# Newton steps with a scalar per partition, and reciprocals written back into PSUM, in a cross-attention and feed-forward kernel

## The chip, the cores and the metric

The kernel runs on one core of a Trainium2 chip. The metric is the device time of one execution in microseconds (us). The core has five engines that each work through a queue of their own: TensorE (PE in the rows; its weight loads are PEld), VectorE (DVE), ScalarE (ACT), GpSimd (POOL) and SyncE (SP), which issues the transfers here.

## The reference

There are 32 batches of 56 query rows, each with 1500 context rows of width 128, 16 heads of width 8. What is computed, cut to what matters:

```python
x = x + xattn(layernorm(x), ctx, ctx, mask, Wq, bq, Wk, bk, Wv, bv, Wo, bo)   # softmax over 1500 keys
x = x + ffn(layernorm(x), w1, w2)

def layernorm(x, eps=1e-5):
    return (x - mean(x)) / sqrt(var(x) + eps)

def ffn(x, w1, w2):                       # rows quantised to 8 bits, weights to -1, 0, 1
    h = gelu(quant_act(x) @ quant_weight(w1).T)
    return quant_act(h) @ quant_weight(w2).T
```

The change touches two places of it: the 1/sqrt(var + eps) of the second layernorm, and the division of the attention's sums by their softmax denominators.

## The kernel before

Everything stays in SBUF; the context and the mask are loaded batch by batch, some steps ahead. A step works on one batch b; an even and an odd step make a pair of batches, whose 112 rows fill one tile. The first pair (batches 0 and 1) and the last pair are written out on their own, and a loop runs the 14 pairs between them. Each engine has its order of work written out by hand as a text of short names (PE_EVEN, DVE_ODD and so on). The names that matter here:

- S (on TensorE; s and f are its opening and closing part) are the scores of a chunk of 125 keys, M the scores that the row maxima are taken from, e their exponentials on ScalarE, P the sums over the values, m the maxima on VectorE.
- T, K and V turn and project the context of a batch that comes later. ScalarE takes T and V out of PSUM.
- own (lines 1101 and 1103) takes each head's sums out of PSUM into `pv_own`. D then has TensorE spread the denominators over the rows of a PSUM bank (line 773), and VectorE takes the reciprocal of the bank into `recip` (line 1045) and multiplies `pv_own` by it into `attn` (line 1047). The bank is given back once line 1047 is done.
- R turns the negated maxima (line 754), and VectorE copies them out as `shift` (line 1021). This copy frees R's bank. SyncE then moves `shift` into `own_query` (line 441), which f needs.
- rows0 and rows1 are the second layernorm and its 8-bit quantisation for the pair before, 112 rows of 128. rows0 calls `statistics` for one tile: mean and variance, then the first guess of 1/sqrt in integer arithmetic (lines 906 to 910), and then three Newton steps of three instructions each (lines 913, 914 and 916). Each of the nine works on one element in each of 112 partitions of `row_stat`, and VectorE waits for each to end before it starts the next. rows1 scales the rows and rounds them (lines 945 to 955) into `row_q`.
- H (line 778) has TensorE turn `row_q`, G and Y are the two layers of the feed-forward part.
- GpSimd makes the low part of the keys (kl, line 574) and the blocks of the queries (q, lines 563 to 567), all of them tensor by tensor in SBUF. Once, in the first pair, it adds the output bias to all rows (line 582).

Seven PSUM banks are handed round in the order of TensorE's slots. At the end of an even step the orders run as follows:

```python
PE_EVEN  ... K2 R0 P1 P2          PE_ODD  V0 T0 H0 s0 M0 f0 S1 S2 M1 ...
DVE_EVEN ... neg0 rows0 R0 rows1 bias2      DVE_ODD  H0 own0 m0 m1 ...
```

By this order the odd step's V0 gets the bank that R0 of the even step has filled, so TensorE can begin V0 only when VectorE has done the copy of line 1021, and this stands behind rows0 in VectorE's queue. The same `statistics` serves the first layernorm, with four tiles at once, at the start of the kernel.

Of the kernel before, what the change touches and what calls it, by code (L numbers as in the profile page):

```python
# [9 lines left out]
ALU = mybir.AluOpType  # L10
# [3 lines left out]
B, SQ, D = 32, 56, 128  # L14
# [189 lines left out]
def xattn_ffn(nc, x, ctx_in, mask, wq, bq, wk, bk, wv, bv, wo, bo, w1, w2, out):  # L204
    es = ExitStack()
    with es:
        def sb(name, shape, dt=F32):
            return es.enter_context(nc.sbuf_tensor(name, shape, dt))

        def sem(name):  # L210
            return es.enter_context(nc.semaphore(name))
# [57 lines left out]
        shift = sb("shift", [NPAIR, 2, SLOT], F32R)  # L269
        probs = sb("probs", [KC, NP, 2, HC])  # L270
        pv_own = sb("pv_own", [128, 2, SQ])
        recip = sb("recip", [128, 2, SQ])
        attn = sb("attn", [128, 2, 2, SQ])

        row_n = w1_sb[0:PAIR, 0:1, :]
# [54 lines left out]
        norm_step = sem("norm_step")  # L330
        attn_ready = sem("attn_ready")
# [25 lines left out]
        def later(bt, n):  # L357
            b, k, p = bt
            return b + n, k + (p + n) // 2, (p + n) % 2

        def wait(e, semaphore, value):

            if not isinstance(value, int) or value > 0:
                e.wait_ge(semaphore, value)
# [13 lines left out]
        def pair_of(st):  # L378

            return st[1] - 1  # L380
# [17 lines left out]
        def wait_bank_full(e, slot, how, st):  # L398
            k = BANK[how][slot]
            e.wait_ge(bank_full[k], fills_before(how, st[1], k) + signalled(how, k).index(slot) + 1)  # L400
# [484 lines left out]
        def _(dve):  # L885
            def chain(semaphore, passed):


                count = 0

                def link(*linked):
                    nonlocal count
                    for ins in linked:
                        ins.then_inc(semaphore, 1)
                    count += len(linked)
                    dve.wait_ge(semaphore, passed + count)
                return link

            def statistics(link, src, st, tiles, room=None):

                link(*[dve.bn_stats(st[:, 0:6, t], src[:, t, :]) for t in range(tiles)])
                if room is not None:

                    dve.memset(room, 0.0)
                link(*[dve.bn_aggr(st[:, 6:8, t], st[:, 0:6, t]) for t in range(tiles)])
                link(dve.tensor_scalar(st[:, 8, :], st[:, 7, :], EPS, None, ALU.add))

                bits = st.bitcast(I32)
                link(dve.tensor_scalar(bits[:, 9, :], bits[:, 8, :], 1, None, ALU.logical_shift_right))
                link(dve.tensor_scalar(bits[:, 9, :], bits[:, 9, :], -1.0, RSQRT_BITS, ALU.mult, ALU.add))  # L910

                for guess, better in ((9, 11), (11, 9), (9, 11)):
                    link(dve.tensor_tensor(st[:, 10, :], st[:, guess, :], st[:, guess, :], ALU.mult))
                    link(dve.scalar_tensor_tensor(out=st[:, 10, :], in0=st[:, 10, :], scalar=-0.5,
                                                  in1=st[:, 8, :], op0=ALU.mult, op1=ALU.mult))
                    link(dve.scalar_tensor_tensor(out=st[:, better, :], in0=st[:, 10, :], scalar=1.5,
                                                  in1=st[:, guess, :], op0=ALU.add, op1=ALU.mult))

            def norm_group(g):

                dve.wait_ge(x_loaded[min(g, 1)], 16)
                if g > 1:
                    dve.wait_ge(xn_copied, g - 1)
                statistics(chain(group_step, 20 * g), x_rows[:, 4 * g:4 * g + 4, :], xn_stat[:], 4)
                for r in range(4):
                    ins = dve.tensor_scalar(xn[:, g % 2, r, :], x_rows[:, 4 * g + r, :], xn_stat[:, 6, r:r + 1],
                                            xn_stat[:, 11, r:r + 1], ALU.subtract, ALU.mult)
                ins.then_inc(xn_ready, 1)
# [80 lines left out]
            def take(slot, how, st):  # L1009
                kind, n = slot  # L1010
                b, k, p = later(st, AHEAD.get(kind, 0))
                t = pair_of(st)
                bank = ps_p[:, BANK[how][kind, n, 0], :]
                wait_bank_full(dve, (kind, n, 0), how, st)
                if kind == "F":
                    wait(dve, q_step, 4 * b - 2)
                    dve.tensor_tensor(q_flag[:], q_all[:, bass.ds(b * SQ, SQ)], bank[:, 0:SQ], ALU.mult)\
                        .then_inc(q_flag_ready, 1)
                elif kind == "R":
                    wait(dve, shift_placed[1 - p], 32 * (k + p))  # L1020
                    dve.tensor_scalar(shift[:].rearrange("j s q -> j (s q)")[:, 0:MROWS], bank[0:NPAIR, 0:MROWS],  # L1021
                                      -1.0 / BIG, None, ALU.mult).then_inc(shift_ready, 1)
                elif kind == "Q":

                    dve.tensor_scalar(q_all[:, n * 4 * PAIR:(n + 1) * 4 * PAIR], bank[:, 0:4 * PAIR],
                                      bq_sb[:, 0:1], float(HD) ** -0.5, ALU.add, ALU.mult).then_inc(q_copied, 1)
                elif kind == "Z":

                    dve.tensor_scalar(wscale[:], bank[:, 0:2], 1.0 / (D * FF), EPS, ALU.mult, ALU.max)\
                        .then_inc(wsum_taken, 1)  # L1030
                    dve.wait_ge(wsum_taken, 1)
                    link = chain(wscale_step, 0)
                    link(dve.reciprocal(wrecip[:], wscale[:]))
                    for w, src in enumerate((w1_sb[:].rearrange("p a i -> p (a i)"), w2_sb[:])):
                        link(dve.tensor_scalar(wtern[:, w, :], src, wrecip[:, w:w + 1], MAGIC, ALU.mult, ALU.add))
                        dve.tensor_scalar(wtern_bf[:, w, :], wtern[:, w, :], MAGIC, 1.0, ALU.subtract, ALU.min)\
                            .then_inc(wtern_ready, 1)
                elif kind == "W":
                    dst = (w1t[:], w2t[:].rearrange("p a o -> p (a o)"))[n]
                    dve.tensor_scalar(dst, bank.bitcast(BF16)[:, 0:FF], -1.0, None, ALU.max).then_inc(wt_copied, 1)  # L1040
                elif kind == "D":

                    if p == 0:
                        wait(dve, x1_ready, k)
                    dve.reciprocal(recip[:].rearrange("p t q -> p (t q)"), bank[:, 0:2 * SQ]).then_inc(norm_step, 1)
                    dve.wait_ge(norm_step, b + 1)
                    dve.tensor_tensor(attn[:, :, p, :], pv_own[:], recip[:], ALU.mult).then_inc(attn_ready, 1)
                elif kind == "B":

                    dve.tensor_tensor(bo_sb[:], bank[0:PAIR, 0:D], bo_sb[:], ALU.add).then_inc(bo_folded, 1)  # L1050
                elif kind == "O":

                    dve.wait_ge(bo_added, 1)
                    if not isinstance(t, int):
                        rows = x_flat[:, bass.ds(t * D, D)]
                    else:
                        rows = x_rows[:, t, :]
                    dve.tensor_tensor(rows, bank[0:PAIR, 0:D], rows, ALU.add).then_inc(x1_ready, 1)
                elif kind == "H":
                    dve.tensor_scalar(row_t[:], bank.bitcast(BF16)[:, 0:PAIR], -128.0, 127.0, ALU.max, ALU.min)\  # L1060
                        .then_inc(row_t_ready, 1)
                elif kind == "U":
                    dve.tensor_scalar(hid_t.rearrange("p a r -> p (a r)"), bank.bitcast(BF16)[:, 0:FF // D * PAIR],
                                      -128.0, 127.0, ALU.max, ALU.min).then_inc(hid_t_ready, 1)
                elif kind == "Y":
                    if not isinstance(t, int):
                        rows = x_flat[:, bass.ds(t * D, D)]
                    else:
                        rows = x_rows[:, t, :]
                    dve.scalar_tensor_tensor(out=rows, in0=bank[0:PAIR, 0:D], scalar=hid_stat[:, 4:5], in1=rows,  # L1070
                                             op0=ALU.mult, op1=ALU.add).then_inc(out_ready, 1)
# [100 lines left out]
```

## Time and profile before

| What | Value |
|---|---|
| time, median of 3 runs (lowest to highest) | 1009.85 us (1007.72 to 1011.45) |
| time of the profiled execution | 1009.53 us |
| its span | 1007.8 us |
| TensorE busy | 908.0 us (90%) |
| VectorE busy | 789.7 us (78%) |
| ScalarE busy | 675.2 us (67%) |
| GpSimd busy | 231.7 us (23%) |
| mean granted TensorE clock | 0.953 of full speed |

The span runs from the first to the last instruction of the profiled execution, and the rest of its time lies around it. Busy time is the time in which an engine runs an instruction. TensorE's clock has two levels, 1.2 and 2.4 GHz, which show as 0.5 and 1.0 in the column of the granted clock.

### The profile page before, as it was taken

What the parts mean: (1) busy time and instruction counts of PE and PEld (TensorE: products, weight loads), DVE (VectorE), ACT (ScalarE), POOL (GpSimd) and SP (SyncE); (2) the same over time, 40 slices, a digit from 0 to 9 for tenths busy, and PEclk for the clock granted to TensorE, in tenths of its full rate; (3) what the DMA queues carried; (4) which work ended last, traced back from release to release, by engine and by line L of the source; (5) the groups of instructions that cost most, each with busy time, mean ns of one, the idle gap of its engine ahead of it and who ended that gap; (6) DMA issues with size and microseconds to landing.
All of it is one profiled execution on the core that took longest, in us unless ns stands there. A gap on an engine that the chain in (4) does not pass through costs nothing.

```text
span 1007.8 us, 33628 instructions
## 1 busy us (share of the span) xinstructions
PE 908.0 (90%) x11716; PEld 712.9 (71%) x11716; DVE 789.7 (78%) x2593; ACT 675.2 (67%) x1272; POOL 231.7 (23%) x253
## 2 busy tenths in 40 slices
PE   3767999999999899999999898998989899998983
PEld 2455767777787777777777777877777777877772
DVE  3786778788888778888788878887887888878854
ACT  2444577767768676767777676776777677687661
POOL 6302042221303222220312222130222213032200
PEclk9789999999999899999999999999999999999996
DMA  5520222101222221112222211122221012220000
GB/s 131 114 59 4 56 60 60 49 27 46 55 57 60 57 56 29 45 47 57 60 57 60 51 35 38 52 57 57 60 57 50 28 44 54 57 60 0 4 2 6
DMA packets 59374, 49.34 MB, mean 49 GB/s; under 512 B 2784, under 2 KB 55632, under 8 KB 59344
## 3 DMA queue, kind: packets, MB, share of 16 engines
q1 hardware_dynamic: 57551, 48.11, 18.1%
q10 hardware_dynamic: 1793, 0.83, 0.3%
q8 instruction: 18, 0.29, 0.1%
q14 instruction: 12, 0.10, 0.0%
HBM read 47.91 MB, written 0.92 MB: 48 GB/s over the span
## 4 chain that ended last, share of the span: by engine, by line
issue 66%; POOL 16%; PE 10%; DVE 5%; ACT 2%; DMA 1%; POOLq 1%; DVEq 0%; ACTq 0%
POOL k_lo L574 7%; POOL qry_hi L566 3%; PE ps_p L821 3%; POOL qry_lo L567 3%; PE ps_v L857 2%; PE ps_p L804 2%; DMA ctx_sb<-in_ctx_dram 1%; DVE max_junk L1083 1%; POOL q_lo L564 1%; POOL q_hi L563 1%; PE ps_p L745 1%; ACT probs L660 1%; DVE mask_bias L996 1%; PE ps_p L759 0%; PE ps_p L742 0%
## 5 line engine op out<-in xcount | busy, mean ns | idle before, releaser
L1083 DVE CUSTOM_DVE_ANT_0 max_junk<-ps_p,mask_bias 120x500 bf16<-120x500 f32 x768 | 481.4, 674 | 136.7 <-PE ps_p L804 115.8
L660 ACT ACTIVATE probs<-ps_p 125x448 f32<-125x448 f32 x768 | 359.9, 550 | 94.0 <-PE ps_p L821 88.8
L574 POOL TENSOR_TENSOR k_lo<-k_full,k_hi 128x500 fp32r<-128x500 f32 x96 | 119.9, 1262 | 643.0 <-ACT k_hi L652 638.3
L821 PE MATMUL ps_p<-qry_hi,k_hi 64*125 64x448 f32 x768 | 163.2, 415 | 3.6 <-DVE seg_max L1083 1.7
L804 PE MATMUL ps_p<-k_hi,qry_hi 64*120 64x500 f32 x768 | 151.7, 420 | 13.0 <-POOL qry_hi L566 5.9
L857 PE MATMUL ps_v<-probs,vals 125*32 125x112 f32 x6144 | 162.9, 262 | 0.5 <-ACT probs L660 0.5
L857 PEld LDWEIGHTS ps_v<-probs,vals 125*32 125x32 f32 x6144 | 146.9, 111 | 20.8 <-issue 17.4
L821 PE MATMUL ps_p<-qry_hi,k_lo 64*125 64x448 f32 x768 | 148.1, 375 | 0.0
L642 ACT ACTIVATE k_full<-ps_p,bk_sb 128x500 f32<-128x500 f32 x96 | 64.8, 675 | 122.9 <-PE ps_p L745 122.4
L821 PE MATMUL ps_p<-qry_lo,k_hi 64*125 64x448 f32 x768 | 147.1, 373 | 0.0
L821 PE MATMUL ps_p<-own_query,mask_bias 57*125 57x448 f32 x768 | 147.0, 372 | 0.0
L749 PE MATMUL ps_p<-wv_sb,ctx_t 128*125 128x128 f32 x768 | 103.9, 283 | 34.3 <-DVE shift L1021 33.6
L749 PEld LDWEIGHTS ps_p<-wv_sb,ctx_t 128*125 128x125 f32 x768 | 92.6, 192 | 44.9 <-DVE shift L1021 37.0
L821 PEld LDWEIGHTS ps_p<-qry_hi,k_hi 64*125 64x125 f32 x768 | 77.0, 191 | 46.4 <-ACT probs L660 15.7
L804 PEld LDWEIGHTS ps_p<-k_hi,qry_hi 64*120 64x120 f32 x768 | 73.5, 186 | 49.0 <-issue 19.9
L745 PE MATMUL ps_p<-ctx_t,wk_sb 128*128 128x500 f32 x192 | 100.9, 620 | 4.1 <-DVE seg_max L1083 4.0
L632 ACT ACTIVATE vals<-ps_p 125x512 f32<-125x512 f32 x96 | 55.6, 597 | 56.7 <-PE ps_p L749 55.1
L821 PEld LDWEIGHTS ps_p<-qry_hi,k_lo 64*125 64x125 f32 x768 | 78.5, 194 | 4.1
L821 PEld LDWEIGHTS ps_p<-qry_lo,k_hi 64*125 64x125 f32 x768 | 77.5, 192 | 5.4
L821 PEld LDWEIGHTS ps_p<-own_query,mask_bias 57*125 57x125 f32 x768 | 76.9, 190 | 5.6 <-DMA own_query<-shift 0.4
L742 PE MATMUL ps_p<-ident,ctx_sb 125*128 125x125 f32 x384 | 61.0, 292 | 16.3 <-DMA ctx_sb<-in_ctx_dram 14.0
L622 ACT ACTIVATE ctx_t<-ps_p 128x500 f32<-128x500 f32 x96 | 54.7, 587 | 15.0 <-PE ps_p L742 12.8
(124 smaller groups left out, 881.0 us busy)
## 6 DMA issues: line engine op xcount, KB each, us to landing
ctx_sb<-in_ctx_dram SPq DMA_DIRECT2D x31, 750.0 KB
mask_sb<-in_mask_Bx1xSxS_ik_dram SPq DMA_DIRECT2D x64, 328.1 KB
own_query<-shift SPq DMA_DIRECT2D x64, 1.8 KB
out_dram<-x_rows SPq DMA_DIRECT2D x16, 56.0 KB, 1.6
ctx_sb<-in_ctx_dram ACTq DMA_DIRECT2D x1, 750.0 KB
x_rows<-in_x_dram SPq DMA_DIRECT2D x1, 672.0 KB, 10.9
w_sb<-in_L_ffn_w_dram SPq DMA_DIRECT2D x2, 256.0 KB, 8.5
x_rows<-in_x_dram SPq DMA_DIRECT2D x1, 224.0 KB, 6.1
```

The costliest lines, as they stand in the source:

```text
L574: pool.tensor_tensor(k_lo[:, p, at], k_full[:, (p + n) % 2, :], k_hi[:, p, at].bitcast(F32), ALU.subtract)\
L622: act.activation(ctx_t[:, p, n * SEG:(n + 1) * SEG], bank[:, 0:SEG], ACT.Copy)\
L632: act.activation(vals[:, p, 4 * n:4 * n + 4, :, 0, :].rearrange("p c v r -> p (c v) r"), bank[0:KC, :].rearrange("p (v r) -> p v r", r=VH) ...
L642: act.activation(k_full[:, (p + n) % 2, :], ps_p[:, BANK[how]["K", n, 0], 0:SEG], ACT.Identity, bias=bk_sb[:, 0:1]).then_inc(k_full_ready, 1)
L660: act.activation(probs[:, c % NP, h], ps_p[0:KC, BANK[how]["S", c, h], 0:HC], ACT.Exp)\
L742: mm = pe.transpose(bank[:, c * KC:(c + 1) * KC], ctx_sb[:, p, 4 * n + c, :], ident[0:KC, 0:KC])
L745: mm = pe.matmul(bank[:, 0:SEG], wk_sb[:], ctx_t[:, p, n * SEG:(n + 1) * SEG], start=True, stop=True)
L749: mm = pe.matmul(bank[0:KC, c * D:(c + 1) * D], ctx_t[:, p, at:at + KC], wv_sb[:], start=True, stop=True)
L804: pe.matmul(ps_p[0:MROWS, BANK[how]["M", n, h], 0:SEG], qry_hi[rows, p, 2 * r:2 * r + 2, :].rearrange("p a q -> p (a q)")[:, 0:MROWS], k_h ...
L821: mm = pe.matmul(ps_p[0:KC, BANK[how]["S", c, h], 0:HC].rearrange("k (a q) -> k a q", a=HH), key[part, :], query[part], start=(n == 0), st ...
L857: mm = pe.matmul(ps_v[r:r + VT, col:col + PAIR], vals[:, p, c, t].rearrange("p a r -> p (a r)"), src, start=(c == 0 and t < 4), stop=(c == ...
L1083: dve.tensor_tensor_reduce(max_junk[0:MROWS, BANK[how][slot], :], ps_p[0:MROWS, BANK[how][slot], 0:SEG], mask_bias[0:MROWS, p, s * SEG:(s ...
```

## The change

The Newton steps of a single tile get a branch of their own. Every instruction that had a second tensor as operand (`tensor_tensor` and `scalar_tensor_tensor`) becomes a `tensor_scalar`, whose second operand is read as one scalar per partition. There are nine instructions as before, with the same waits between them. In D, the reciprocal is written over the denominators in their PSUM bank instead of into `recip`, and the product reads the bank and `pv_own`; `recip` goes away. The four-tile form at the start is as before.

```diff
-        recip = sb("recip", [128, 2, SQ])
...
+                if tiles == 1:
+
+                    for guess, better in ((9, 11), (11, 9), (9, 11)):
+                        link(dve.tensor_scalar(st[:, 10, :], st[:, guess, :], st[:, guess, :], None, ALU.mult))
+                        link(dve.tensor_scalar(st[:, 10, :], st[:, 10, :], st[:, 8, :], -0.5, ALU.mult, ALU.mult))
+                        link(dve.tensor_scalar(st[:, better, :], st[:, 10, :], 1.5, st[:, guess, :],
+                                               ALU.add, ALU.mult))
+                    return
...
-                    dve.reciprocal(recip[:].rearrange("p t q -> p (t q)"), bank[:, 0:2 * SQ]).then_inc(norm_step, 1)
+                    dve.reciprocal(bank[:, 0:2 * SQ], bank[:, 0:2 * SQ]).then_inc(norm_step, 1)
                     dve.wait_ge(norm_step, b + 1)
-                    dve.tensor_tensor(attn[:, :, p, :], pv_own[:], recip[:], ALU.mult).then_inc(attn_ready, 1)
+                    dve.tensor_tensor(attn[:, :, p, :], bank[:, 0:2 * SQ].rearrange("p (t q) -> p t q", t=2),
+                                      pv_own[:], ALU.mult).then_inc(attn_ready, 1)
```

## Rows read from the trace of the kernel before

**Rows 1.** Waits of TensorE: us in total, times, longest.

```profile
PE ps_p L749 <- DVE shift L1021: 33.6, 14, 2.4
PE ps_p L778 <- DVE w_sb L955: 9.0, 10, 5.2
```

**Rows 2.** Timeline of TensorE, one loop pair: start, us, line, operation [idle before].

```profile
503.90 3.27 PE L857 MATMUL ps_v<-probs,vals 125*32 125x112 f32 x128
...
509.59 1.17 PE L749 MATMUL ps_p<-wv_sb,ctx_t 128*125 128x128 f32 x8 [2.41 <-DVE shift L1021]
...
511.44 0.27 PE L778 MATMUL ps_p<-ident_bf,w_sb 112*128 112x112 bf16 x1
```

**Rows 3.** Timeline of VectorE, same stretch.

```profile
503.47 0.15 DVE L910 TENSOR_SCALAR row_stat<-row_stat 112x1 int32<-112x1 int32 x1
503.65 0.97 DVE L913 TENSOR_TENSOR row_stat<-row_stat 112x1 f32<-112x1 f32 x1
...
507.29 1.16 DVE L916 SCALAR_TENSOR_TENSOR row_stat<-row_stat 112x1 f32<-112x1 f32 x1
...
509.26 0.27 DVE L1021 TENSOR_SCALAR shift<-ps_p 8x120 fp32r<-8x120 f32 x1 [0.23 <-DVE row_stat L916]
509.46 0.32 DVE L945 TENSOR_SCALAR w_sb<-x_rows,row_stat 112x128 f32 x1
...
511.16 0.23 DVE L955 TENSOR_SCALAR w_sb<-w_sb 112x128 bf16<-112x128 f32 x1
```

**Rows 4.** Timeline of GpSimd, same stretch.

```profile
503.46 1.14 POOL L566 TENSOR_TENSOR qry_hi<-head_of_row,q_hi 128x448 fp32r<-128x448 f32 x1 [0.17 <-POOL q_lo L564]
...
505.99 2.45 POOL L574 TENSOR_TENSOR k_lo<-k_full,k_hi 128x500 fp32r<-128x500 f32 x2 [0.16 <-POOL qry_lo L567]
```

**Rows 5.** Stretches of 5 us, first and last of 14: busy by engine, granted clock, DMA.

```profile
161.96:166.96 5.00, 5.00 (x31) 4.35 (x31) 3.30 (x13) 1.70 (x4) 0.00 (x0) 0.66 0.13 37
...
914.88:919.88 5.00, 4.68 (x29) 4.13 (x31) 3.50 (x15) 1.60 (x4) 0.00 (x0) 0.69 0.00 1
```

**Rows 6.** Instructions on the tile row_stat: ns min/median/max, first and last start.

```profile
L913 DVE TENSOR_TENSOR row_stat<-row_stat x48: 159/160/969, 156.0 to 996.7; 112x1 f32<-112x1 f32 x48
...
L910 DVE TENSOR_SCALAR row_stat<-row_stat x16: 153/153/155, 155.8 to 995.3; 112x1 int32<-112x1 int32 x16
...
L950 DVE TENSOR_SCALAR row_stat<-row_stat,wscale x16: 214/214/215, 162.7 to 998.1; 112x1 f32<-112x1 f32 x16
```

**Rows 7.** Timelines of GpSimd and VectorE at the end of an odd step.

```profile
534.27 1.25 POOL L574 TENSOR_TENSOR k_lo<-k_full,k_hi 128x500 fp32r<-128x500 f32 x1 [25.84 <-ACT k_hi L652]
...
535.01 0.35 DVE L1070 SCALAR_TENSOR_TENSOR x_rows<-ps_p,hid_stat,x_rows 112x128 f32 x1
535.28 0.52 DVE L996 TENSOR_SCALAR mask_bias<-mask_sb 121x500 fp32r<-121x500 int32 x1
```

**Rows 8.** Timeline of TensorE where V and T run at full clock.

```profile
537.14 1.04 PE L749 MATMUL ps_p<-wv_sb,ctx_t 128*125 128x128 f32 x8
538.02 1.02 PE L742 MATMUL ps_p<-ident,ctx_sb 125*128 125x125 f32 x8
```

**Rows 9.** Timeline of TensorE in the last pair, then that stretch with its clock.

```profile
970.18 0.22 PE L778 MATMUL ps_p<-ident_bf,w_sb 112*128 112x112 bf16 x1 [1.44 <-DVE w_sb L955]
...
970.00:972.00 2.00, 1.82 (x17) 1.74 (x19) 0.92 (x4) 0.42 (x1) 0.00 (x0) 1.00 0.00 1
```

**Rows 10.** Timelines of VectorE and TensorE, a shift of an odd step and its use.

```profile
537.34 0.27 DVE L1021 TENSOR_SCALAR shift<-ps_p 8x120 fp32r<-8x120 f32 x1 [0.47 <-PE ps_p L754]
...
541.19 0.38 PE L821 MATMUL ps_p<-own_query,mask_bias 57*125 57x448 f32 x2
```

**Rows 11.** The reciprocal of D by form: shapes, count, us in total, mean ns, idle before.

```profile
L1045 DVE RECIPROCAL recip<-ps_p 128x112 f32<-128x112 f32 x32 | 27.2, 849 | 0.6 <-PE ps_p L773 0.6
```

**Rows 12.** Timelines of VectorE and TensorE at the end of the first pair.

```profile
127.62 3.71 DVE L1047 TENSOR_TENSOR attn<-pv_own,recip 128x112 f32<-128x112 f32 x1
...
131.70 1.09 PE L742 MATMUL ps_p<-ident,ctx_sb 125*128 125x125 f32 x4 [2.38 <-DVE q_flag L1017]
```

## The prediction

> **What bounds the kernel now.** The table of busy times comes first: TensorE is busy for 90% of the span, every other engine for much less, so an idle stretch of TensorE costs time unless something else is late anyway. The second view is therefore the list of TensorE's waits [rows 1]. Its longest entry is V waiting for the copy of line 1021: 14 times, 2.4 us each, 33.6 us in all, once in each of the 14 loop pairs. The third view is the timeline of one loop pair, engine by engine. TensorE ends its sums over the values at 503.90 + 3.27 = 507.17 and can go on at 509.59 [rows 2]. VectorE meanwhile stands in the Newton steps, which begin at 503.65; the copy starts only at 509.26 [rows 3]. Why do nine one-element instructions take 5.4 us? The first ends at 504.62, and GpSimd's instruction beside it at 504.60; one of the later ones, started at 507.29, ends at 508.45, and GpSimd's last at 508.44 [rows 3, 4]. So an instruction that reads two tensors in SBUF is held until GpSimd's running instruction ends. The last view is the granted clock: in the 5 us after each wait its mean is 0.66 to 0.69, that is, the lower of the two levels (0.5) for about 3.4 us [rows 5]. With TensorE busy throughout, this costs another (1 - 0.66) x 5 = 1.7 us per pair. The wait and the clock together are 14 x (2.4 + 1.7) = 57 us.
>
> **The Newton steps.** Nine instructions go, nine come. With GpSimd idle an old one takes 0.16 us (the minimum); the nearest row for a new one is line 950, a one-element instruction with a scalar per partition in SBUF and an immediate, 0.214 us in all 16 cases [rows 6]. From the end of one to the start of the next linked one it is 0.03 us (503.47 + 0.15 to 503.65 [rows 3]). So nine new ones take 9 x 0.245 = 2.2 us where none is held. None is held if two things are true. First, a one-element instruction with one tensor must not be held: line 910 runs beside GpSimd's instruction from 503.46 on and takes 0.15 us [rows 3, 4], and 153 to 155 ns in all 16 cases [rows 6]. Second, the scalar must not count as a second tensor: line 1070 reads a bank, a tensor in SBUF and a scalar in SBUF, and ends within 0.35 us in the middle of GpSimd's 1.25 us [rows 7]. No row has a tensor and a scalar both in SBUF, with GpSimd reading beside it, so the bounds are 2.2 us and the old 5.4 us with a little more; I take 2.2, because the row with the scalar is nearest.
>
> In the loop the steps then end at 503.65 + 2.2 = 505.9 and the copy, 0.23 us later as now, runs from 506.1 to 506.4. TensorE asks for it at 507.17, so that wait disappears, with 0.8 us to spare.
>
> The Trainium skill has a rule that speaks against this (SBUF — State Buffer, section "Who interferes with whom"): a tensor_scalar from SBUF to SBUF can enter a mode in which it uses both of VectorE's ports, and then it too contends with GpSimd. For one element the rows of line 910 show nothing of it; for long ones line 996 shows it, and by the rule the new steps would be held as the old ones are, which is the fourth case below.
>
> **What is late next.** rows1 now starts some 3 us earlier and falls beside GpSimd's two k_lo (505.99 to 508.44 [rows 4]). Its long instructions go from SBUF to SBUF, as line 996 does, and line 996 is held: started at 535.28, it ends at 535.80, 0.28 us after GpSimd's 535.52 [rows 7]. So I let line 945, which would start at 506.3, wait for the first k_lo and end at about 507.2 + 0.2 = 507.4. From the end of line 945 (509.46 + 0.32 = 509.78) to that of line 955 (511.39) it is 1.61 us now [rows 3]; the long ones in it come at about 508.4, where GpSimd ends. `row_q` is ready at 507.4 + 1.6 = 509.0, and H can start 0.05 us later. TensorE would like it when V0 and T0 are done. At full clock V takes 0.88 us for eight matmuls (537.14 to 538.02 [rows 8]), so V0 and T0's four take 0.88 + 0.44 = 1.3 us: 507.17 + 1.3 = 508.5. That leaves **a new wait of 0.6 us** before H (bounds: 0 if line 945 is not held, 1.8 if it is held by both k_lo).
>
> Does the clock still fall? In the last pair TensorE waits 1.44 us for the same H, and the granted clock in that stretch is 1.00 [rows 9]. A wait of 0.6 us is shorter than that, so I count the 1.7 us as gained.
>
> After H comes f0, which needs the shift in `own_query`. An odd step's copy ends at 537.61, and its f0 begins at 541.19, 3.6 us later and without a wait [rows 10]. The new f0 stands 3.7 us behind the new copy (506.4; f0 about 1 us behind H's 509.1), so this transfer stays hidden, though with little room. On SyncE's queue the next loads stand behind the transfer of the shift, and all of them come earlier with it.
>
> **D.** The reciprocal takes 0.85 us now [rows 11]. No row has VectorE writing PSUM, so its cost can move either way; I take 0.2 us as the bound on both sides, about a quarter of it, an estimate. The product reads a bank and a tensor, like line 1070 (0.35 us with a scalar and 128 elements), so it keeps its length and is no longer held by GpSimd. In the loop's odd step the shift's copy behind D waits another 0.47 us for TensorE [rows 10], which covers it; in the even step the attention rows are wanted some microseconds later. I cost D at 0; if the cover were gone it would be at most 32 x 0.2 = 6 us. Once it gains: at the end of the first pair the old product is held for 3.71 us, and TensorE then waits 2.38 us on VectorE's queue behind it [rows 12]. GpSimd's bias addition, which holds it, also holds up the query blocks that are wanted next, so I take 1 us of this (bounds 0 and 2.4 + 1.7).
>
> **The ends.** In the last pair and in the tail GpSimd is idle, and TensorE waits for rows1 (1.44 us in [rows 9], 5.2 us the longest in [rows 1]). There nine steps cost 9 x (0.214 - 0.160) = 0.5 us more each time, 1 us in all.
>
> **The sum**, against the profiled execution's 1009.5 us (0.3 us under the median, so the two can be read as one): per loop pair 2.4 + 1.7 - 0.6 = 3.5, times 14 = 49. Eight of the pairs have a wait for H already, 9.0 - 5.2 - 1.4 = 2.4 us in all [rows 1], which the 0.6 replaces: 51.4. Plus 1 for the first pair, minus 1 for the ends: 1009.5 - 51.4 = **958 us**.
>
> **The rivals.** (1) The wait goes but the clock still falls, since the new wait before H stands where the old one stood. For it: the fall has followed the wait in all 14 pairs. Against it: [rows 9]. It gives back 14 x 1.7: 982 us. (2) rows1 is held by both k_lo, H waits 1.8 us, and the clock falls: 982 + 14 x 1.2 = 999 us. Against it: the old Newton steps got through between GpSimd's instructions, one ending at 508.45 after starting at 507.29. (3) Something else is late at once, such as the shift's transfer behind f0 or ScalarE's turn at T0, and most of the gain is lost: within 0.5%, about 1007 us. Against it: after the wait TensorE waits for neither in the odd step. (4) **Slower**: the scalar, or the tensor_scalar itself, goes through the port that GpSimd holds. Then the steps are held as before, and the unheld ones among them cost 0.05 us more each: 0.2 us per pair and 1 us at the ends, about 1013 us. If GpSimd won every turn until 508.44, all nine would follow: 508.44 + 2.2 = 510.6 in place of 509.0, 14 x 1.6 + 1, about 1033 us. It decides against the change as soon as the first new step is held for more than GpSimd's current instruction. In this case the part of the change in the Newton steps doesn't do what it says. Against it: lines 910 and 1070.
>
> **How the numbers follow.** Forecast 958: 0.66. (1) 982: 0.14. (2) 999: 0.06. (3) 1007: 0.05. (4) 0.09, about half of it within 0.5% and half above. The range runs from 948 (no wait before H, 14 x 0.6 = 8 us, and 2 us more in the first pair) to 984 (the first rival and D's bounds); what is left out is 0.2. A measurement of this kernel can tell about 0.5% (5 us) from no change. Faster by more: 0.66 + 0.14 + 0.06 = 0.86; within: 0.05 + 0.04 = 0.09; slower: 0.05.
>
> **What would show it.** In the profile of the changed kernel: every Newton step at about 0.21 us, beside GpSimd too; no wait of V for line 1021; a wait of 0.3 to 0.8 us of H for line 955, 14 times; line 945 longer than 0.33 us in the loop; a granted clock near 1.0 in the loop; a loop pair that is 3.5 to 3.8 us shorter than before. Newton steps of about 1 us mean the fourth case; a clock of 0.66 after H the first; a wait of TensorE under another name the third.

## The result

The changed kernel takes 959.8 us in the median (959.6 to 959.8), the kernel before 1009.2; the ratio is 0.951, 95% interval 0.949 to 0.953. The profiled execution took 959.8 us with a span of 958.0. The forecast was 958.

The first view of the changed kernel is the list of TensorE's waits, which answers to [rows 1] (us in total, times, longest). Lines of the changed kernel lie up to 8 off those of the kernel before: line 748 is V, 777 H, 1028 the shift's copy, 962 the end of rows1, 803 M.

```profile
PE ps_p L777 <- DVE w_sb L962: 11.7, 16, 5.7
PE ps_p L803 <- POOL qry_hi L565: 6.5, 4, 2.9
```

No wait of V for the shift's copy is left; it had been 33.6 us. H waits for rows1 in all 16 pairs, where it had waited in 10: the two at the end are 5.73 and 1.93 us, so the loop's 14 share 4.0 us, 0.29 us each.

The timelines of one loop pair show how that comes about. VectorE first, the answer to [rows 3], then GpSimd beside it [rows 4] (start, us, line, operation, idle before):

```profile
481.83 0.21 DVE L914 TENSOR_SCALAR row_stat<-row_stat 112x1 f32<-112x1 f32 x1
...
483.82 0.21 DVE L916 TENSOR_SCALAR row_stat<-row_stat 112x1 f32<-112x1 f32 x1
484.26 0.27 DVE L1028 TENSOR_SCALAR shift<-ps_p 8x120 fp32r<-8x120 f32 x1 [0.23 <-DVE row_stat L916]
484.46 1.03 DVE L952 TENSOR_SCALAR w_sb<-x_rows,row_stat 112x128 f32 x1
...
486.87 0.23 DVE L962 TENSOR_SCALAR w_sb<-w_sb 112x128 bf16<-112x128 f32 x1
```

```profile
481.63 1.14 POOL L565 TENSOR_TENSOR qry_hi<-head_of_row,q_hi 128x448 fp32r<-128x448 f32 x1 [0.16 <-POOL q_lo L563]
482.85 1.15 POOL L566 TENSOR_TENSOR qry_lo<-head_of_row,q_lo 128x448 fp32r<-128x448 f32 x1
484.15 2.46 POOL L573 TENSOR_TENSOR k_lo<-k_full,k_hi 128x500 fp32r<-128x500 f32 x2 [0.16 <-POOL qry_lo L566]
```

The nine steps take 2.2 us (481.83 to 484.03), although GpSimd runs beside all of them. The copy follows 0.23 us later. Then the first instruction of rows1 is held: 1.03 us in place of 0.33, until 485.49, 0.1 us after the first low-key instruction (half of 2.46 us, from 484.15 on).

TensorE in the same pair, the answer to [rows 2]:

```profile
482.10 3.27 PE L856 MATMUL ps_v<-probs,vals 125*32 125x112 f32 x128
485.31 1.14 PE L748 MATMUL ps_p<-wv_sb,ctx_t 128*125 128x128 f32 x8
486.28 0.59 PE L741 MATMUL ps_p<-ident,ctx_sb 125*128 125x125 f32 x4
487.15 0.22 PE L777 MATMUL ps_p<-ident_bf,w_sb 112*128 112x112 bf16 x1 [0.28 <-DVE w_sb L962]
487.46 0.47 PE L820 MATMUL ps_p<-qry_hi,k_hi 64*125 64x448 f32 x2
```

V follows the sums over the values at once. The granted clock is the fifth view; these are stretches of 5 us from H on in the first and the last loop pair (length, busy time with counts of PE, PEld, DVE, ACT and POOL, then the granted clock), against 0.66 and 0.69 in [rows 5]:

```profile
161.37:166.37 5.00, 4.83 (x45) 4.26 (x47) 3.49 (x11) 3.71 (x10) 0.00 (x0) 1.00 0.30 91
866.33:871.33 5.00, 4.92 (x45) 4.36 (x47) 3.61 (x12) 3.81 (x10) 0.00 (x0) 1.00 0.00 0
```

Two groups by tile and by form (ns min/median/max; count, us in total, mean ns) answer to [rows 6] and [rows 11]:

```profile
L914 DVE TENSOR_SCALAR row_stat<-row_stat x48: 213/214/217, 156.0 to 946.7; 112x1 f32<-112x1 f32 x48
```

```profile
L1052 DVE RECIPROCAL ps_p<-ps_p 128x112 f32<-128x112 f32 x32 | 27.4, 857 | 0.6 <-PE ps_p L772 0.6
L1054 DVE TENSOR_TENSOR attn<-ps_p,pv_own 128x112 f32<-128x112 f32 x32 | 8.8, 275 | 1.1
```

Every one of the steps takes 0.21 us. Writing the reciprocal to PSUM costs 857 ns against 849 to SBUF.

Whole times differ by some us between executions, and a part of this lies ahead of the loop: in the first 150 us the mean granted clock is 0.91 in the profiled executions of the kernel before and of the changed one, and 0.84 to 0.92 in those of the kernels below. The loop is the better measure. The table gives, for each kernel of the study, the time between rows0 of the first and of the 14th loop pair (start of the instruction that puts the variance together), divided by 13.

| Kernel | Median us | From, to (us) | Loop pair (us) |
|---|---|---|---|
| before | 1009.2 | 155.25, 908.16 | 57.92 |
| changed | 959.8 | 155.27, 860.23 | 54.23 |
| newton_only | 963.6 | 160.51, 864.97 | 54.19 |
| d_only | 1007.6 | 153.43, 903.61 | 57.71 |
| newton_two_wide | 1014.5 | 154.79, 910.84 | 58.16 |
| h_after_s | 967.0 | 161.58, 869.56 | 54.46 |
| kl_written_only | 959.8 | 152.28, 862.59 | 54.64 |
| after_kl_written_only | 951.0 | 153.61, 850.46 | 53.60 |
| late_by_11 | 978.8 | 160.43, 880.96 | 55.43 |
| late_by_16 | 1002.8 | 153.35, 896.78 | 57.19 |
| rows1_one_port | 957.8 | 154.92, 857.70 | 54.06 |
| changed_again | 959.8 | 155.05, 859.49 | 54.19 |
| both_one_port | 954.5 | 154.61, 853.88 | 53.79 |
| changed_third | 959.8 | 156.43, 860.80 | 54.18 |

### The profile page after: what moved, and what is told of

It reads as the page before. It is cut to its first block, busy times and chain, and to the rows that moved or that the text cites. A ratio compares the mean times of both kernels' runs of the same rounds, so it can differ in the third digit from the quotient of the medians.

```text
span 958.0 us, 33628 instructions
## 1 busy us (share of the span) xinstructions
PE 887.8 (93%) x11716; PEld 694.2 (72%) x11716; DVE 753.1 (79%) x2593; ACT 673.4 (70%) x1272; POOL 231.5 (24%) x253
## 4 chain that ended last, share of the span: by engine, by line
issue 66%; POOL 18%; PE 7%; DVE 5%; ACT 1%; DMA 1%; POOLq 1%; DVEq 0%; ACTq 0%
POOL k_lo L573 8%; POOL qry_hi L565 4%; POOL qry_lo L566 4%; PE ps_p L820 2%; DMA ctx_sb<-in_ctx_dram 1%; PE ps_p L803 1%; DVE max_junk L1091 1%; POOL q_lo L563 1%; POOL q_hi L562 1%; PE ps_v L856 1%; PE ps_p L744 1%; ACT probs L659 1%; POOL x_rows L581 0%; PE ps_p L741 0%; POOLq L556 0%
## 5 line engine op out<-in xcount | busy, mean ns | idle before, releaser
L803 PE MATMUL ps_p<-k_hi,qry_hi 64*120 64x500 f32 x768 | 148.8, 413 | 15.6 <-POOL qry_hi L565 6.5
L820 PE MATMUL ps_p<-qry_hi,k_hi 64*125 64x448 f32 x768 | 158.6, 403 | 4.4 <-DVE seg_max L1091 1.7
L820 PE MATMUL ps_p<-qry_lo,k_hi 64*125 64x448 f32 x768 | 144.4, 366 | 0.0
L820 PE MATMUL ps_p<-qry_hi,k_lo 64*125 64x448 f32 x768 | 144.3, 365 | 0.0
L748 PE MATMUL ps_p<-wv_sb,ctx_t 128*125 128x128 f32 x768 | 100.9, 278 | 0.7 <-DVE seg_max L1091 0.7
L748 PEld LDWEIGHTS ps_p<-wv_sb,ctx_t 128*125 128x125 f32 x768 | 90.1, 188 | 10.3 <-issue 9.0
L820 PEld LDWEIGHTS ps_p<-qry_lo,k_hi 64*125 64x125 f32 x768 | 74.9, 185 | 5.2
L820 PEld LDWEIGHTS ps_p<-qry_hi,k_lo 64*125 64x125 f32 x768 | 75.4, 186 | 4.1
L741 PE MATMUL ps_p<-ident,ctx_sb 125*128 125x125 f32 x384 | 57.7, 282 | 13.8 <-DMA ctx_sb<-in_ctx_dram 13.8
L1091 DVE DVE_READ_ACCUMULATOR2_ANT seg_max<- 120x1 f32 x768 | 63.8, 83 | 0.0
```

The source lines that it names most:

```text
L741: mm = pe.transpose(bank[:, c * KC:(c + 1) * KC], ctx_sb[:, p, 4 * n + c, :], ident[0:KC, 0:KC])
L748: mm = pe.matmul(bank[0:KC, c * D:(c + 1) * D], ctx_t[:, p, at:at + KC], wv_sb[:], start=True, stop=True)
L803: pe.matmul(ps_p[0:MROWS, BANK[how]["M", n, h], 0:SEG], qry_hi[rows, p, 2 * r:2 * r + 2, :].rearrange("p a q -> p (a q)")[:, 0:MROWS], k_h ...
L820: mm = pe.matmul(ps_p[0:KC, BANK[how]["S", c, h], 0:HC].rearrange("k (a q) -> k a q", a=HH), key[part, :], query[part], start=(n == 0), st ...
L1091: dve.tensor_tensor_reduce(max_junk[0:MROWS, BANK[how][slot], :], ps_p[0:MROWS, BANK[how][slot], 0:SEG], mask_bias[0:MROWS, p, s * SEG:(s ...
```

## The experiments

The theory: a Newton step that reads two tensors in SBUF is held by GpSimd, the change takes the holding away, TensorE's wait goes with it, and the clock, which fell because of the wait, stays up. Rivals: D brings a part of it; the width or the form of the steps matters and not the holding; the clock fell for a reason of its own.

**Each part alone.** The first kernel keeps D as before:

```diff
-        dve.reciprocal(bank[:, 0:2 * SQ], bank[:, 0:2 * SQ]).then_inc(norm_step, 1)
+        dve.reciprocal(recip[:].rearrange("p t q -> p (t q)"), bank[:, 0:2 * SQ]).then_inc(norm_step, 1)
...
+        dve.tensor_tensor(attn[:, :, p, :], pv_own[:], recip[:], ALU.mult).then_inc(attn_ready, 1)
```

> The Newton steps as scalars per partition, the reciprocal of D into recip and the product from two SBUF tensors as before the change. Theory (the Newton steps carry the loop's whole gain, D only the first pair): 960.5 to 962 us, the loop as in the changed kernel, the product at the end of the first pair held for 3.7 us again and TensorE waiting 2.4 us there. Rival (writing PSUM costs VectorE time that shows): below 959 us. Rival (D carries a part of the loop's gain): above 965 us.

Measured: 963.6 us, ratio 0.954 (0.951 to 0.957), the loop pair 54.19 us as in the changed kernel. The whole time is 2 us above what was expected, at the start: its first rows0 comes 5 us later than the changed kernel's (160.51 for 155.27), and the mean granted clock of the first 150 us is 0.85 there against 0.91. At the end of the first pair TensorE waits 2.37 us on VectorE's queue again. The product from two SBUF tensors in this kernel in this kernel (ns min/median/max, first and last start):

```profile
L1055 DVE TENSOR_TENSOR attn<-pv_own,recip x32: 274/275/3709, 131.1 to 947.7; 128x112 f32<-128x112 f32 x32
```

The one long product in 32, 3.7 us, is the one at the end of the first pair, beside GpSimd's addition of the bias. In the loop it is 0.275 us with either form.

The second kernel has only D's part:

> Only D as in the change (reciprocal written into its PSUM bank), the Newton steps as before. Theory: 1007.5 to 1009 us, the 14 waits for line 1021 at 2.4 us as before, one wait of 2.4 us in the first pair gone. The reciprocal between 0.65 and 1.05 us. Rival (D carries a part of the loop's gain): below 1003 us.

Measured: 1007.6 us, ratio 0.999 (0.996 to 1.001), the 14 waits of V at 2.4 us each as before, 57.71 us per pair. The interval holds 1, so no gain from D is shown. That the loop pair is 0.21 us shorter than before comes from two single pairs: after the wait that ends at 738.53 the clock stays at 1.00 here (56.61 us from V to V), and in the kernel before the pair from 335.03 on has a lower clock for twice as long as the others (59.32 us). Without these two, both kernels take 57.80 us from V to V. In the first pair D gains nothing that shows either: TensorE's wait of 2.38 us is gone, but one of 2.88 us for the query blocks stands in its place, and from GpSimd's bias addition to the first rows0 it is 29.0 us, where it was 28.7 before (126.51 to 155.25). So the Newton steps carry the gain.

**The form or the holding?** Here the steps keep the form of the change, but eight of the nine work on two elements per partition:

```diff
-    link(dve.tensor_scalar(st[:, 10, :], st[:, guess, :], st[:, guess, :], None, ALU.mult))
+    link(dve.tensor_scalar(wide[:, 2:4], wide[:, guess:guess + 2], wide[:, guess:guess + 1], None, ALU.mult))
...
```

> The changed kernel, but eight of the nine Newton steps work on two elements per partition, the second of them an unused zero. Theory A (a tensor_scalar over two elements from SBUF to SBUF takes both of VectorE's ports and is held by GpSimd as the old steps were): steps of about 1 us beside GpSimd, the wait of V for the shift back at 2.4 to 3 us, the clock down after it, 1008 to 1014 us. Theory B (one tensor from SBUF is never held, however wide): steps of 0.21 us, 960 us.

Measured: 1014.5 us, ratio 1.007 (1.004 to 1.009): the whole gain is gone. The timelines of VectorE and of GpSimd in one pair:

```profile
505.39 0.97 DVE L917 TENSOR_SCALAR wide<-wide 112x2 f32<-112x2 f32 x1
506.40 1.19 DVE L919 TENSOR_SCALAR wide<-wide,row_stat 112x2 f32<-112x2 f32 x1
507.62 0.23 DVE L921 TENSOR_SCALAR wide<-wide 112x2 f32<-112x2 f32 x1
507.89 1.12 DVE L917 TENSOR_SCALAR wide<-wide 112x2 f32<-112x2 f32 x1
```

```profile
505.20 1.14 POOL L567 TENSOR_TENSOR qry_hi<-head_of_row,q_hi 128x448 fp32r<-128x448 f32 x1 [0.17 <-POOL q_lo L565]
506.42 1.15 POOL L568 TENSOR_TENSOR qry_lo<-head_of_row,q_lo 128x448 fp32r<-128x448 f32 x1
507.72 2.46 POOL L575 TENSOR_TENSOR k_lo<-k_full,k_hi 128x500 fp32r<-128x500 f32 x2 [0.16 <-POOL qry_lo L568]
```

The first step ends at 506.36, GpSimd's instruction beside it at 506.34; the second at 507.59 and 507.57. One more element per partition costs 0.02 us where nothing holds the step, and about 1 us where GpSimd runs. So it isn't the scalar operand by itself that frees the steps: it is the scalar operand on a single element. This kernel does what rival (4) of the prediction says; V waits 2.85 to 2.90 us in it, and the clock falls after all 14 waits.

**What of GpSimd holds them.** In the kernel before, the low keys are written as zeros, but for the first column of each part; the scores lack them (`first` stands for that column, `rest` for the other 499):

```diff
-    pool.tensor_tensor(k_lo[:, p, at], k_full[:, (p + n) % 2, :], k_hi[:, p, at].bitcast(F32), ALU.subtract)
+    pool.tensor_tensor(k_lo[:, p, first], k_full[:, (p + n) % 2, 0:1], k_hi[:, p, first].bitcast(F32), ALU.subtract)
+    pool.memset(k_lo[:, p, rest].bitcast(F32), 0.0)
```

> The kernel before the change, but GpSimd writes zeros into the low part of the keys (one column is still subtracted), so that it reads next to nothing there; the scores lack this part. Theory (what holds a two-tensor Newton step is GpSimd's reading of SBUF, and it is gone as soon as no reading instruction runs): the steps beside the two query blocks are held, those beside the zeros take 0.16 us, the chain ends some 3.4 us after its start in place of 5.4, the wait of V falls from 2.4 to about 0.4 us, the clock stays up, 960 to 970 us. The mask's bias at the end of the odd step, 0.53 us beside the low keys now, shows whether a two-port instruction is held by mere writes. Rival (any GpSimd instruction holds them): steps of 0.3 to 0.5 us beside the zeros. Rival (the form of the steps alone made them slow): 1009 us.

Measured: 959.8 us (two runs, 958.9 and 960.6), 54.64 us per pair; V waits 0.4 us in place of 2.4, and the clock doesn't fall in the loop. VectorE's and GpSimd's timelines:

```profile
482.11 1.00 DVE L919 SCALAR_TENSOR_TENSOR row_stat<-row_stat 112x1 f32<-112x1 f32 x1
...
483.53 0.16 DVE L919 SCALAR_TENSOR_TENSOR row_stat<-row_stat 112x1 f32<-112x1 f32 x1
```

```profile
481.94 1.15 POOL L567 TENSOR_TENSOR qry_lo<-head_of_row,q_lo 128x448 fp32r<-128x448 f32 x1
...
483.37 0.52 POOL L578 MEMSET k_lo<- 128x499 f32 x1
```

The step at 482.11 is held by the query block, which reads; the one at 483.53, wholly beside the writing of zeros (483.37 to 483.89), takes 0.16 us. The old two-tensor form is then almost as good as the new one. So it was the holding, and a GpSimd instruction that only writes doesn't hold a step with two tensors.

The same on the changed kernel:

> The changed kernel, with the low part of the keys written as zeros in the same way; the scores lack it. Theory (the first instruction of rows1, 1.03 us now, is held by GpSimd's low keys, and TensorE's last wait of 0.29 us for H comes from this alone): it takes 0.33 us, or some 0.5 us if writes hold it too, H waits no more, 14 x 0.29 = 4 us less than the changed kernel. Rival (something else in rows1 is late): H waits as before.

Measured: 951.0 us (two runs, 948.4 to 953.7), 53.60 us per pair, 0.63 less than the changed kernel, and H waits in the two last pairs only. rows1's first instruction in one pair, with GpSimd beside it:

```profile
478.76 0.52 POOL L577 MEMSET k_lo<- 128x499 f32 x1
```

```profile
478.94 0.42 DVE L955 TENSOR_SCALAR w_sb<-x_rows,row_stat 112x128 f32 x1
```

It ends at 479.36, 0.08 us after the zeros at 479.28, and is 0.09 us longer than alone (0.40 to 0.43 us in all 14 pairs, 0.33 where GpSimd is idle): a long tensor_scalar from SBUF to SBUF is held by mere writes as well, unlike the two-tensor steps. The gain per pair is twice the wait of 0.29 us. TensorE's weight loads waited longer for H than its matmuls did; their waits for H, first in the run changed_again, then here:

```profile
PEld ps_p L777 <- DVE w_sb L962: 15.5, 16, 6.0
```

```profile
PEld ps_p L780 <- DVE w_sb L965: 8.2, 2, 6.0
```

The difference is 7.3 us, 0.52 per loop pair. TensorE's own timeline shows the whole: here the first scores begin 481.32 - 479.75 = 1.57 us after V, in the changed kernel 487.46 - 485.31 = 2.15. So H being late costs 0.6 us per pair, of which the list of the matmuls' waits shows 0.29.

```profile
479.75 1.14 PE L751 MATMUL ps_p<-wv_sb,ctx_t 128*125 128x128 f32 x8
...
481.15 0.21 PE L780 MATMUL ps_p<-ident_bf,w_sb 112*128 112x112 bf16 x1
481.32 0.46 PE L823 MATMUL ps_p<-qry_hi,k_hi 64*125 64x448 f32 x2
```

**What a late shift costs.** The changed kernel gets idle work on VectorE between the Newton steps and the shift's copy, in the loop only, where nothing holds it:

```diff
+    for n in range(11):          # 16 in the second kernel
+        dve.tensor_reduce(late[:, n:n + 1], ones_f[:], AX.X, ALU.add)
```

> The changed kernel with 11 reductions of 128x128 (some 0.2 us each, 2.2 us) put behind the Newton steps of the loop's 14 pairs; their results are not used. Nothing is held by GpSimd then. Theory (only the length of TensorE's idle time decides what a late shift costs): V waits some 1.3 us for the shift, the clock stays at 1.0, 14 x 1.5 = 21 us more than the changed kernel, about 981 us. Rival (a wait at this place brings the clock down whatever its length): 14 x 1.7 more, about 1005 us.

> The same with 16 reductions, some 3.2 us. Theory: V waits 2.3 to 2.4 us as in the kernel before, although no Newton step is held, the granted clock after it is 0.66 to 0.7 again, and the time comes back to 1008 to 1020 us: the wait and the clock are the whole of the old cost. Rival (the clock fell for another reason in the old steps): clock near 1.0, about 996 us.

Measured: 978.8 (two runs, 976.5 to 981.1) and 1002.8 us. TensorE's waits for the shift, first with 11, then with 16:

```profile
PE ps_p L749 <- DVE shift L1032: 16.2, 14, 1.2
```

```profile
PE ps_p L749 <- DVE shift L1032: 29.7, 14, 2.1
```

With 11, V waits 1.13 to 1.18 us in each pair and the clock never falls in the loop. The loop pair is 55.43 - 54.23 = 1.20 us longer, which is the wait and nothing else. With 16, V waits 2.11 to 2.14 us, and the clock falls after 11 of the 14 waits. Two stretches of 5 us from V on in this kernel, one of the three without a fall and one with it:

```profile
332.23:337.23 5.00, 4.62 (x39) 4.03 (x41) 3.99 (x16) 2.56 (x6) 0.00 (x0) 1.00 0.13 38
503.24:508.24 5.00, 4.68 (x29) 4.15 (x31) 3.50 (x15) 1.60 (x4) 0.00 (x0) 0.68 0.13 39
```

So a wait on TensorE brings the clock down even where no Newton step is held: 11 times in 14 at 2.1 us, never at 1.1 us. What a fall costs can be read within this kernel. From V to the next V it takes 56.33 to 56.37 us in the three pairs without one, and 57.31 to 57.68 us, 57.44 in the mean, in the ten with one (behind the 14th pair no V of the loop follows): 1.1 us for each. The time stayed below the 1008 us expected, because V waits 2.1 us where 2.3 to 2.4 were expected, and three falls are missing.

**Three tries at the last waits.** First TensorE's order: the opening of the first scores ahead of H in the odd step, ahead of M0 in the even one.

```diff
-    V0 T0 H0 s0 M0 f0 S1 S2 ...    # odd
+    V0 T0 s0 H0 M0 f0 S1 S2 ...
-    T0 T1 V0 M0 s0 f0 M1 ...       # even
+    T0 T1 V0 s0 M0 f0 M1 ...
```

> The changed kernel with two slots of TensorE's order moved: in the odd step the opening of the first scores ahead of H, in the even step ahead of M0. Theory (TensorE is what bounds the loop, so its last waits are worth their length): the waits of 0.29 us for rows1 and 0.26 us for the query blocks go, 14 x 0.55 = 7.7 us less, about 952 us. Rival (VectorE or ScalarE, which get H and M later, become late instead): 958 to 962 us, with new waits of TensorE under other names.

Measured: 967.0 us, 54.46 us per pair, so the rival, with more lost than it said. The loop accounts for 14 x 0.23 = 3.2 us of the loss; the rest lies ahead of it (first rows0 at 161.58 for 155.27, with a mean clock of 0.84 in the first 150 us for 0.91). The longest waits of TensorE in this kernel after the first load:

```profile
PE ps_p L820 <- ACT probs L659: 10.4, 31, 0.6
```

The loop's waits for rows1 and for the query blocks, 14 x 0.55 = 7.7 us, went, and scores now wait 31 times for ScalarE's exponentials, whose end frees their bank: 10.4 us. The banks are handed round in the order of the slots, so a slot that is moved changes who waits for whom.

Second, rows1's first scaling in a form that also writes a sum. In this form the second operation only makes the sum, so the rows are not multiplied by 1/std.

```diff
-    ALU.subtract, ALU.mult))
+    ALU.subtract, ALU.mult, accum_out=unread[:]))
```

> The changed kernel, but the first instruction of rows1 also writes out a sum per partition that nobody uses, which leaves the form that is held. Theory (it is held because a long tensor_scalar from SBUF to SBUF uses both ports, and that is all that H waits for): it takes 0.4 to 0.5 us beside GpSimd in place of 1.03, TensorE's wait for H goes, 14 x 0.29 = 4 us less than the changed kernel run beside it, about 956 us. Rival (held all the same): 960 us.

> The changed kernel itself, on the same chip as the run before it, to compare with: 958 to 964 us.

Measured: 957.8 us (ratio 0.949, 0.946 to 0.953) against 959.8 (0.952, 0.949 to 0.954), 54.06 us per pair against 54.19. The whole times can't be told apart; the loop is 0.13 us per pair shorter. VectorE's timeline in one pair, and GpSimd's:

```profile
482.58 0.39 DVE L953 TENSOR_SCALAR_CACHE_REDUCE w_sb<-x_rows,row_stat 112x128 f32 x1
...
484.02 0.79 DVE L962 TENSOR_SCALAR w_sb<-w_sb,row_stat 112x128 f32<-112x128 f32 x1
```

```profile
482.27 2.46 POOL L574 TENSOR_TENSOR k_lo<-k_full,k_hi 128x500 fp32r<-128x500 f32 x2 [0.16 <-POOL qry_lo L567]
```

The first scaling is no longer held, but the second now comes 0.7 us earlier, falls beside the second low-key instruction and is held until it ends at 484.73. Most of the gain is given back at once.

Third, both scalings in that form, with 1/std multiplied into the scalars, so that the whole of the reference is computed with the same number of steps:

```diff
-    link(dve.tensor_scalar(row_n[:, 0, :], src[:, 0, :], row_stat[:, 6:7], row_stat[:, 11:12], ALU.subtract, ALU.mult))
+    link(dve.tensor_scalar(row_n[:, 0, :], src[:, 0, :], row_stat[:, 6:7], None, ALU.subtract, ALU.add, accum_out=unread[:]))
...
-    link(dve.tensor_scalar(row_stat[:, 15:16], row_stat[:, 14:15], 127.0, None, ALU.mult))
-    link(dve.tensor_scalar(row_scaled, row_n[:, 0, :], row_stat[:, 15:16], None, ALU.mult))
+    link(dve.tensor_scalar(row_stat[:, 15:16], row_stat[:, 14:15], 127.0, row_stat[:, 11:12], ALU.mult, ALU.mult))
+    link(dve.tensor_scalar(row_scaled, row_n[:, 0, :], row_stat[:, 15:16], None, ALU.mult, ALU.add, accum_out=unread[:]))
```

> The changed kernel with both long scalings of rows1 in the form that also writes a sum (nobody uses it), and 1/std multiplied into the scalars instead of the rows, so that the whole of the reference is computed with the same number of steps. Theory (TensorE's wait for H comes from GpSimd holding one or the other of these two): the two take 0.35 to 0.45 us each beside GpSimd, H waits no more, a loop pair takes 53.6 to 53.9 us in place of 54.2, 4 to 8 us less than the changed kernel, 952 to 956 us. Rival (something else in rows1, or TensorE itself, ends last): 54.2 us per pair, 958 to 962 us.

> The changed kernel again beside it, to compare with: 958 to 963 us, 54.2 us per loop pair.

Measured: 954.5 us, ratio 0.949 (0.945 to 0.952), against 959.8 us, ratio 0.953 (0.950 to 0.956), for the changed kernel beside it. The two intervals overlap, but the loop shows the difference: 53.79 us per pair against 54.18 (54.18 to 54.23 in the three executions of the changed kernel), which is 14 x 0.39 = 5.5 us, about the distance of the medians. The two scalings by form (count, us in total, mean ns, idle before), and H's waits:

```profile
L964 DVE TENSOR_SCALAR_CACHE_REDUCE w_sb<-w_sb,row_stat 112x128 f32<-112x128 f32 x16 | 5.5, 346 | 0.6
L953 DVE TENSOR_SCALAR_CACHE_REDUCE w_sb<-x_rows,row_stat 112x128 f32 x14 | 4.5, 325 | 0.0
```

```profile
PE ps_p L778 <- DVE w_sb L966: 8.0, 2, 5.9
```

Neither is held, and the list shows H waiting in the two last pairs only. It is still a little late: the first scores begin 483.36 - 481.61 = 1.75 us after V, for 1.57 with the zeros, which is the 0.2 us between 53.79 and 53.60. This is the fastest of the kernels that compute the whole.

## Why the prediction was right

The forecast was 958 us, and 959.8 was measured. The mechanism of the loop holds at each link. That the sum comes within 2 us is partly luck: two of its terms had the wrong size, and they cancel. Step by step:

- **Two-tensor steps are held by GpSimd.** Right, and shown: the same old steps take 0.16 us beside a GpSimd that only writes (kl_written_only).
- **The new steps take 0.214 us, unheld.** Right: 213 to 217 ns, and the chain takes 2.2 us. The Trainium skill (VectorE: DVE Perf Modes, section "Mode 2×_2P — use both read ports for one tensor") asks, for the mode in which a tensor_scalar uses both ports, for an outermost dimension longer than one that is even, or odd and the same in source and destination; one element has no such dimension, two elements have one. The pair of kernels with one and with two elements agrees: 0.21 us against 0.97 to 1.19 us beside GpSimd. The rule weighed in the prediction thus holds, but from the second element on; the prediction had left out this condition.
- **The wait of V goes.** Right: none is left.
- **A new wait of H, 0.6 us.** The size is right, but it is no new cost. The hold was as forecast (line 952 ends 0.1 us after the first low-key instruction, rows1 1.6 us later), and the scores behind H come 0.6 us later than with nothing late (2.15 us after V, 1.57 in after_kl_written_only). But in the kernel before they came 511.75 - 509.59 = 2.16 us after V, and H began 0.05 us after the end of rows1 there too (511.39 and 511.44, [rows 2] and [rows 3]; so in 10 of the 14 pairs, while in the four others the clock fell sooner and H came later still): in the old kernel rows1 was as late behind V as in the new one. I had taken the old lateness from the list of waits, 2.4 us in all, and the list doesn't show it in the pair of [rows 2]. So the term to subtract was near 0, not 0.6.
- **1.7 us for the clock.** Mechanism right, size too large: 1.1 to 1.2 us. The fall follows a wait without any held step (late_by_16), and it goes when the wait does. I had taken half of the whole 3.4 us at the lower level. In the pair of [rows 2] the granted clock is 1.00 from 510.0 to 510.5, 0.50 from 511.0 to 513.5 and 1.00 again from 514.0. The scores begin at 511.75, no later behind V than in the changed kernel at full clock (2.16 and 2.15 us), so what lies ahead of them costs nothing: there TensorE waits for rows1 in any case. Of the 3.4 us some 2.2 come behind them and cost half of that, 1.1 us. The row of the scores in the kernel before:

```profile
511.75 0.74 PE L821 MATMUL ps_p<-qry_hi,k_hi 64*125 64x448 f32 x2
```

- **The sum of a loop pair, 3.5 us.** Measured: 57.92 - 54.23 = 3.69 us. From the end of the sums over the values to the start of V it was 509.59 - 507.17 = 2.42 us and now V begins 0.06 us ahead of the end that the profile gives them (485.31 and 485.37), together 2.48; the 1.21 us that remain are what the clock costs. I had 2.4 + 1.7 - 0.6, and with the 2.4 us of old waits for H shared out over the pairs 3.67: the clock 0.5 us too large, H 0.4 too large the other way.
- **D at nothing in the loop, 1 us in the first pair.** Right for the loop: newton_only's loop is the changed kernel's, and the reciprocal is 8 ns longer, where I had allowed 200. The 1 us in the first pair is not there: TensorE now waits 2.88 us for the query blocks that GpSimd makes after its addition of the bias, in place of 2.38, and from the bias addition to the first rows0 it is 29.1 us for 28.7 (126.21 to 155.27, 126.51 to 155.25). The blocks were named in the prediction, but their price was put too low.
- **The shift's transfer stays hidden.** Right: no f0 of the loop waits for it.
- **The ends, 0.5 us each.** The waits are as forecast: 1.93 us for 1.44 and 5.73 for 5.22. But after the wait of 1.93 us the clock falls in the profiled execution (0.66 in the 5 us from 918.96 on), which I had not counted; in the run changed_again it stays at 1.00 after the same wait. From the 14th rows0 to the end of the span it was 1007.8 - 908.16 = 99.6 us and is 958.0 - 860.23 = 97.8, with the 3.7 us of the 14th pair in it, so the ends cost 1.8 us in place of 1.

The parts add up: 14 x 3.69 - 1.8 = 49.9 us, and the two profiled executions lie 1009.5 - 959.8 = 49.7 us apart; the forecast was 51.4.

Of the rivals, the clock's staying down and the double hold didn't come. The wait of another name (H) is no dearer than what stood there before. Rival (4) exists on this chip and needs one more element.

## What to carry to other kernels

Where VectorE's small instructions take a microsecond in place of 0.16 us and end together with GpSimd's, look at how many operands they read from SBUF, and count what TensorE waits for behind them. Three things let the instruction pass here: a scalar operand on a single element (0.21 us), an operand in PSUM (the product of D takes 0.28 us beside GpSimd's bias addition, 3.71 us from two SBUF tensors), and, for a long tensor_scalar, the form that also writes a sum. A chain that is made shorter brings what follows it under the next GpSimd instruction, so look there before counting the gain. Where TensorE's clock falls after a wait, count both, but the fall only by the work that follows the clock. And read what a late instruction costs from the distance between two fixed points of TensorE's timeline, before and after, not from the list of waits alone.

## What the runs showed of the hardware that was not expected

- A held VectorE instruction gets its turn between two GpSimd instructions that follow each other without a gap: line 952 ends 0.1 us after the first of two low-key instructions, in 14 pairs of 14.
- GpSimd's mere writes hold a long tensor_scalar from SBUF to SBUF (0.40 to 0.43 us for 0.33, ending 0.08 us after the writes) and don't hold an instruction with two SBUF tensors (0.16 us).
- The form that also writes a sum is not held (325 to 346 ns beside the low keys), though it reads and writes the same 112x128 elements as the form that is held for 0.7 us.
- A fall of TensorE's clock for 3.4 us cost 1.1 to 1.2 us. Waits of V of 1.13 to 1.18 us brought none in 14 (late_by_11), of 2.11 to 2.14 us 11 in 14 (late_by_16), of 2.4 us 14 in 14 in the kernel before and 13 in 14 in d_only, and of 2.85 to 2.90 us 14 in 14 (newton_two_wide). So a wait of the same length can bring a fall or not.
